# Building the adjacency counts of a graph: how the edge keys are written and loaded, and which engine casts a part of them

## The reference

```python
edge_index = jnp.stack([src, dst])
h = jnp.maximum(_layernorm(x, axis=-1), 0.0)
x = x + _L0_gnn_ref(h, src, dst, ...)          # two degree-normed convolutions
h = jnp.maximum(_layernorm(x, axis=-1), 0.0)
x = x + _L1_gnn_ref(h, src, dst, ...)          # two mean aggregations with weights
h = jnp.maximum(_layernorm(x, axis=-1), 0.0)
x = x + _L2_gnn_ref(h, edge_index, ...)        # two attention layers
h = jnp.maximum(_layernorm(x, axis=-1), 0.0)
x = x + _L3_gnn_ref(h, edge_index, 3125)
```

## Time and profile before

| | |
|---|---|
| median of 3 runs | 802.03 us (800.73 to 803.16) |
| the profiled execution's own time | 800.52 us |
| its span | 798.7 us |
| granted TensorE clock, mean of the span | 0.932 |
| PE busy | 700.2 us, 88% |
| DVE busy | 570.8 us, 71% |
| ACT busy | 409.6 us, 51% |
| POOL busy | 39.2 us, 5% |

### The profile page before, as it was taken

The page is one execution under the profiler, slowest core; times in us unless marked ns, Lnnn a source line. Parts: engine busy times, 40 slices in busy tenths (PEclk is TensorE's granted clock), DMA queues, the critical chain, the costliest instruction groups (busy, mean ns, idle before and its releaser), DMA issues. The chain is left out here.

```text
span 798.7 us, 18765 instructions
## 1 busy us (share of the span) xinstructions
PE 700.2 (88%) x7841; PEld 658.5 (82%) x7841; DVE 570.8 (71%) x1273; ACT 409.6 (51%) x699; POOL 39.2 (5%) x30
## 2 busy tenths in 40 slices
PE   6078888789998999999999759999963999997997
PEld 6066655569997999999999749999953999996997
DVE  6198999995355545533444689999878999996732
ACT  6236666661004123222132778999566899974600
POOL 6001352000000000000000000000000000000000
PEclk8688999989998999999999979999965999999999
DMA  5000000006990000000000412666661099997811
GB/s 138 22 1 20 7 7 6 1 2 219 413 412 9 1 2 2 2 2 2 1 27 14 128 37 73 216 213 200 210 214 35 19 207 217 217 178 206 167 28 35
DMA packets 121203, 78.05 MB, mean 98 GB/s; under 512 B 97793, under 2 KB 115905, under 8 KB 120986
## 3 DMA queue, kind: packets, MB, share of 16 engines
q1 hardware_dynamic: 120446, 75.33, 33.1%
q0 software_dynamic: 384, 0.94, 0.4%
q10 hardware_dynamic: 284, 0.51, 0.2%
HBM read 30.51 MB, written 25.78 MB: 70 GB/s over the span
## 5 line engine op out<-in xcount | busy, mean ns | idle before, releaser
L1998 PE MATMUL banks<-loose,adjacency 128*128 128x194 f16 x1250 | 211.9, 247 | 0.0
L773 PE MATMUL banks<-y_sb,adjacency 128*128 128x192 f16 (+1 forms) x1875 | 166.2, 249 | 0.8 <-DVE h_sb L1020 0.8
L773 PEld LDWEIGHTS banks<-y_sb,adjacency 128*128 128x128 f16 x1875 | 161.7, 99 | 1.5 <-DVE h_sb L1020 1.0
L1997 PE MATMUL banks<-x_sb,gat_masks 128*128 128x194 f16 x820 | 141.0, 248 | 2.3 <-DVE adjacency L1912 2.2
L1968 ACT ACTIVATE gat_masks<-y_sb,node_scalars 128x640 bf16<-128x640 f32 x164 | 121.8, 826 | 4.0 <-PEq L135 4.0
L1998 PEld LDWEIGHTS banks<-loose,adjacency 128*128 128x128 f16 x1250 | 122.4, 98 | 0.3
L714 ACT ACTIVATE adjacency<-counts 128x850 f16<-128x850 f32 x92 | 81.0, 880 | 69.6 <-PE counts L607 67.7
L1997 PEld LDWEIGHTS banks<-x_sb,gat_masks 128*128 128x128 f16 x820 | 80.3, 98 | 3.2 <-DVE y_sb L1908 2.6
L1908 DVE TENSOR_TENSOR gat_masks<-gat_masks,adjacency 128x1920 f16<-128x1920 bf16 (+1 forms) x64 | 64.2, 1006 | 6.6 <-ACT gat_masks L1968 6.4
L1251 ACT ACTIVATE y_sb<-banks 96x256 f32<-96x256 f32 x50 | 19.1, 381 | 93.7 <-PE banks L1283 93.7
L431 DVE TENSOR_TENSOR hot_codes<-codes_iota,unpacked 128x2016 f16<-128x2016 f16 (+5 forms) x76 | 65.3, 909 | 0.2
(11 more groups left out here) (283 smaller groups left out, 1096.8 us busy)
## 6 DMA issues: line engine op xcount, KB each, us to landing
kept_adj<-adjacency SPq DMA_DIRECT2D x5, 4000.0 KB, 31.8
adjacency<-kept_adj SPq DMA_DIRECT2D x25, 800.0 KB, 9.2
y_sb<-a_dst_rows SPq DMA_DIRECT2D x10, 320.0 KB, 3.7
residual<-h_sb SPq DMA_DIRECT2D x5, 240.0 KB, 2.0
kept_x<-x_sb SPq DMA_DIRECT2D x1, 1200.0 KB, 5.1
loose<-residual SPq DMA_DIRECT2D x5, 240.0 KB, 3.6
x_sb<-kept_x SPq DMA_DIRECT2D x5, 240.0 KB, 4.9
x_sb<-in_x SPq DMA_DIRECT2D x4, 240.0 KB
```

The costliest lines, as they stand in the source:

```text
L773: return nc.tensor.matmul(k.ps[:, j % G, 0:cols], k.ADJ[:, i, j * P:(j + 1) * P], y[:, i, 0:cols], start=i == 0, stop=i == NT - 1)
L1997: nc.tensor.matmul(bank[:, 0:2 * BC], over_of(x)[:, q * P:(q + 1) * P], features[0][:, i, :], start=i == 0, stop=False)
L1998: return nc.tensor.matmul(bank[:, 2 * BC:4 * BC], under_of(x)[:, q * P:(q + 1) * P], features[1][:, i, :], start=False, stop=i == NT - 1)
```

## The change

- The write of the keys is cut into three: rows 0 to 47 (`first_keys_out`), 48 to 111 and 112 to 124 (`keys_out`), with each row as one run of 1600 numbers.
- `dst_first` has 112 rows of 250, is loaded first of all, by SyncE's queue, and has a semaphore of its own. DVE does all of the early bases and `early_after` before it turns to `src`; ACT does four of the seven early Sign steps ahead of `dst_scaled`. The early edges come ahead of the main bases.
- The early starts of load 0 and load 1 are summed and released one by one; PE waits for the first before it computes the second.
- DVE's wait for `keys_out` moves from before `unpack(0)` to before `unpack(1)`, after octet 0.
- For loads from the third on, the cast of line 422 goes to ACT, after it has stored the pair that follows the load's turn; DVE waits for it in `unpack`.
- `degree` starts at pair 14, two products after even pairs and one after odd ones, until it has caught up. The main beginnings run over pairs 2 to 9 in quarters of a tile, the shifts over 10 to 13.
- Small: `trouble` is cleared first, its three tests move, `place_of` is waited for.

```diff
-BEGINS_AT, SPLIT_AFTER, SPREAD_AT, STARTS_AFTER, TURN_AT = 4, 3, 8, 4, 17
+BEGINS_AT, BEGINS_IN, SPLIT_AFTER, SPREAD_AT, STARTS_AFTER, TURN_AT = 2, 4, 3, 10, 4, 17
+DEGREES_FROM = 14
-EARLY_EDGES = 224
-FIRST_KEYS = -(-(EP * EARLY_EDGES + P) // EF)
+EARLY_PARTS, EARLY_EDGES = 112, 250
+FIRST_KEYS = 48
+SIGNS_FIRST = 4
...
-    key_writes = 16 * 2
+    key_writes = 16 * 3
...
     def _(sp):
+        sp.dma_start(dst_first, d.dst[0:EARLY_PARTS * EARLY_EDGES].rearrange("(p f) -> p f", p=EARLY_PARTS)).then_inc(first_in, 16)
...
-        for some, done in ((slice(0, FIRST_KEYS), first_keys_out), (slice(FIRST_KEYS, EP), keys_out)):
-            sp.dma_start(d.keys[some.start * EF:some.stop * EF, :].rearrange("(p f) e -> p f e", f=EF),
-                         pairs_f[some, :, :]).then_inc(done, 16)
+        for some, done in ((slice(0, FIRST_KEYS), first_keys_out), (slice(FIRST_KEYS, EVEN), keys_out), (slice(EVEN, EP), keys_out)):
+            sp.dma_start(d.keys[some.start * EF:some.stop * EF, :].rearrange("(p f) e -> p (f e)", f=EF),
+                         pairs_flat[some, :]).then_inc(done, 16)
...
-            pool.wait_ge(starts_ready, 1 if load < EARLY_LOADS else 2)
+            pool.wait_ge(starts_ready, min(load, EARLY_LOADS) + 1)
...
+        def bases(n, parts, first, bias, most):
+
+            chain(dve.tensor_scalar(base_i[0:parts, n:n + 1], first, DIVIDE, None, ALU.mult))
+            chain(dve.tensor_scalar(base_i[0:parts, n:n + 1], base_i[0:parts, n:n + 1], SHIFT, None, ALU.logical_shift_right))
+            chain(dve.tensor_scalar(node_of[0:parts, n:n + 1], base_i[0:parts, n:n + 1], float(W), None, ALU.mult))
+            dve.tensor_scalar(bias[0:parts, :], step_nodes[0:parts, 0:most], node_of[0:parts, n:n + 1], 0.5, ALU.add,
+                              ALU.subtract).then_inc(bias_ready, 1)
+            chain(dve.tensor_scalar(place_of[0:parts, n:n + 1], base_i[0:parts, n:n + 1], float(WT), None, ALU.mult))
...
+        dve.wait_ge(first_in, 16)
+        bases(1, EARLY_PARTS, dst_first[:, 0:1], early_bias, EARLY_STEPS)
+        dve.tensor_scalar(early_after[0:EARLY_PARTS, :], places[0:EARLY_PARTS, 0:LEADING + WT * EARLY_WINDOWS], place_of[0:EARLY_PARTS, 1:2],
+                          None, ALU.is_gt).then_inc(edges_ready, 1)
         dve.wait_ge(src_in, 32)
...
+        dve.wait_ge(signed, EARLY_STEPS)
+        edges_of(EARLY_PARTS, early_signs, early_edges, EARLY_STEPS)
+        dve.wait_ge(dst_in, 32)
+        bases(0, EP, dst[:, 0:1], main_bias, MAIN_STEPS)
...
+        for load in range(EARLY_LOADS):
+            starts_of(slice(load, load + 1), early_starts_ps, load + 1)
...
-            chain.later(dve.tensor_copy(unpacked[:, load % 2, 0, 0:n, :], keys_ps[:, 0:n].unsqueeze(2).to_broadcast([P, n, 2])))
+            if load < EARLY_LOADS:
+                chain.later(dve.tensor_copy(unpacked[:, load % 2, 0, 0:n, :], rows_of(load)))
+            else:
+                dve.wait_ge(rows_cast, load - EARLY_LOADS + 1)
...
-        dve.wait_ge(keys_out, key_writes)
         unpack(0)
...
                 if o == 0:
+                    dve.wait_ge(keys_out, key_writes)
                     unpack(1)
...
         for n in range(EARLY_LOADS):
-            last = start(early_starts_ps[:, 2 * n:2 * n + 2], n, 1, EARLY_WINDOWS)
-        last.then_inc(starts_summed, 1)
+            if n > 0:
+                pe.wait_ge(starts_ready, n)
+            start(early_starts_ps[:, 2 * n:2 * n + 2], n, 1, EARLY_WINDOWS).then_inc(starts_summed, 1)
         keep_busy(BUSY_NEXT)
...
-            if p >= LATER:
-                degree(p - LATER)
-            if BEGINS_AT <= p < BEGINS_AT + 4:
+            if p >= DEGREES_FROM:
+                for _ in range(2 - p % 2):
+                    if degrees_done <= p - LATER:
+                        degree(degrees_done)
+                        degrees_done += 1
+            if BEGINS_AT <= p < BEGINS_AT + 2 * BEGINS_IN:
...
-                if p == (TURN_AT if load == 1 else FIRST[load] // 2 + 1):
+                if p == turned_at(load):
                     turn(load + 1)
...
-        act.dma_start(dst_first, d.dst[0:EP * EARLY_EDGES].rearrange("(p f) -> p f", p=EP)).then_inc(dst_in, 16)
         act.preload_act_table(ACT.Sign)
-        act.wait_ge(dst_in, 48)
...
+        act.wait_ge(bias_ready, 1)
+        signs_from(dst_first, early_bias, early_signs, range(0, SIGNS_FIRST), EF)
+        act.wait_ge(dst_in, 32)
         nc.scalar.activation(dst_scaled, dst, ACT.Copy, scale=HALF * NT).then_inc(scaled_ready, 1)
...
+        signs_from(dst_first, early_bias, early_signs, range(SIGNS_FIRST, EARLY_STEPS), EF)
...
+            for load in range(EARLY_LOADS, len(LOADS)):
+                if p == turned_at(load - 1) + 1:
+                    act.wait_ge(keys_turned, load + 1)
+                    act.wait_ge(rows_hot, FIRST[load - 1] // OCT)
+                    nc.scalar.activation(unpacked[:, load % 2, 0, 0:LOADS[load] * WT, :], rows_of(load), ACT.Copy).then_inc(rows_cast, 1)
```

More of the change, by code:

```diff
@@ L203, in build_adjacency @@
     dst, src, row_i, tile_i = (early(t, I32, EF) for t in range(4))
-    dst_scaled, dst_first = early(4, F32, EF), early(5, I32, EARLY_EDGES)
+    dst_scaled, dst_first = early(4, F32, EF), early(5, I32, EARLY_EDGES)[0:EARLY_PARTS, :]
     pads = k.ADJ[0:1, 7, 0:4 * P].bitcast(F32)
-    pairs_f = k.h_memory[0:EP, 0:2 * EF].rearrange("p (f e) -> p f e", e=2)
+    pairs_flat = k.h_memory[0:EP, 0:2 * EF]
+    pairs_f = pairs_flat.rearrange("p (f e) -> p f e", e=2)
     def kept(t, n):
@@ L221, in build_adjacency @@
     total_ps = keys_ps[0:1, 0:NT + 3]
+    first_in = sem("first_in")
     dst_in, src_in, x_in, keys_out = sem("dst_in"), sem("src_in"), sem("x_in"), sem("keys_out")
@@ L243, in build_adjacency, with turned_at, rows_of @@
     block = c.enter_context(nc.Block())
-    key_writes = 16 * 2
+    def turned_at(load):
+        return TURN_AT if load == 1 else FIRST[load] // 2 + 1
+    def rows_of(load):
+        n = LOADS[load] * WT
+        return keys_ps[:, 0:n].unsqueeze(2).to_broadcast([P, n, 2])
+    key_writes = 16 * 3
     octs = NW // OCT
@@ L342, in _ @@
             chain.later(dve.memset(edges[:, WT + n:], 0.0))
+        chain.later(dve.memset(trouble[:, :], 0.0))
         chain.later(dve.memset(halves[:, :, :, :], 0.0))
@@ L349, in _, with edges_of @@
         chain.all()
[L351 to L357, removed]
+        def bases(n, parts, first, bias, most):
[5 more added lines that the diff above has]
+            chain(dve.tensor_scalar(place_of[0:parts, n:n + 1], base_i[0:parts, n:n + 1], float(WT), None, ALU.mult))
+        def edges_of(parts, signs_of, edges, n):
+            return dve.tensor_tensor(edges[0:parts, WT - 1:WT + n], signs_of[0:parts, 1:n + 2], signs_of[0:parts, 0:n + 1],
+                                     ALU.subtract).then_inc(edges_ready, 1)
+        dve.wait_ge(first_in, 16)
+        bases(1, EARLY_PARTS, dst_first[:, 0:1], early_bias, EARLY_STEPS)
+        dve.tensor_scalar(early_after[0:EARLY_PARTS, :], places[0:EARLY_PARTS, 0:LEADING + WT * EARLY_WINDOWS], place_of[0:EARLY_PARTS, 1:2],
+                          None, ALU.is_gt).then_inc(edges_ready, 1)
         dve.wait_ge(src_in, 32)
@@ L556, in _, with begin @@
         keep_busy(BUSY_FIRST)
-        def begin(out, after, edges, n, tile, windows, some):
+        def begin(out, parts, after, edges, n, tile, windows, some):
             for at in some:
@@ L562, in begin @@
                 first = LEADING + WT * TILE_WINDOWS * tile - lag
-                last = nc.tensor.matmul(out, after[0:EP, first:first + WT * (windows - 1) + 1:WT], edges[0:EP, at:at + WT],
+                last = nc.tensor.matmul(out, after[0:parts, first:first + WT * (windows - 1) + 1:WT], edges[0:parts, at:at + WT],
                                         start=at == 0, stop=at == n + WT - 1, skip_group_check=True)
@@ L652, in stay_busy @@
                 nc.tensor.matmul(counts[:, 0, 0:P], k.ident_h[:, :], k.ident_h[:, :], start=True, stop=True)
-        for p in range(PAIRS - LATER, PAIRS):
+        for p in range(degrees_done, PAIRS):
             last = degree(p)
```

65 lines of the change are left out of this document (25 added, 40 removed).

## The result

The changed kernel takes 779.72 us in the median of four runs (779.62 to 780.21) against 801.38 us before (798.61 to 803.16): a ratio of 0.9734, 95% interval 0.9705 to 0.9763. The forecast was 779.5 in a range of 775.5 to 786. The profiled execution's span fell from 798.7 to 777.9 us.

The account below looks back on a forecast made before the run. VectorE's 16.8 us wait for the keys' write was taken to bound the matrix building. Gains of 17.65 (start), 2.8 (PE waits) and 1.3 (cast) sum to 21.75 us, giving 778.8 to 780.3; forecast 779.5, range 775.5 to 786.

Parts of the forecast that it names:

- What bound the kernel: Building of the matrix: VectorE waits 16.8 us before the first unpacking for the keys' write, 89 rows in one DMA engine.
- The start: Up to VectorE's unpacking of load 0: at 18.9 us instead of 36.55, a gain of 17.65 us.
- The chain: Steps making the first load: bases 4.3, early edges 9.7, first starts 12.25, gather issued 13.4 and landed 17.4 us.
- `keep_busy`, not the transfer, is late next: Before load 0's transposes: the idle PE products end between 17.7 and 18.4 us, later than the gather at 17.4.
- both my ends of 4.7 and 5.41: Durations in us for the 45 idle products: 4.7 at 0.104 each, 5.41 as in the kernel before.
- my bound of 18.4: Before load 0's transposes: the latest end in us forecast for the 45 idle products, the earliest being 17.7.
- The octet after it: After load 0: the moved wait for the keys comes at 25.1 us; keys and main Signs are ready, nothing held up.
- The old waits for PE: In the counting: VectorE's two waits for PE, 2.8 us together, are removed; ends 0.8 and 2.8.
- The cast: In the counting: ACT's casts save VectorE 1.5 us, the third load loses 0.2 net; gain 1.3, ends 0 and 1.8.
- the write was spread: Keys' write: the rival said 64 rows still use one DMA engine, start gain 10 us, 787 us; chance 0.05.
- the late chain: Rival at the start: `dst_first` lands late or the gather is longest, VectorE starts at 22 to 23.7, 782.5 to 784.5; chance 0.14.
- PE at the lower clock: Rival in the counting: PE idles at 1.2 GHz and sets the pace, 25 us lost, about 803; chance 0.03.

Follow-up runs that it names:

- the even pieces alone: The kernel before, with only the writes of the keys cut into 48, 64 and 13 rows: 785.62 us, ratio 0.982.
- the old ones: The changed kernel with the two old writes of the keys, rows 0 to 35 and 36 to 124: 789.5 us, ratio 0.9892.
- 61 rows: The changed kernel with the second write of the keys cut at 61 rows and the third with 16: 786.27 us.
- The first profile: Profile of the changed kernel's first group of runs, against the kernel before; median 779.72 us, ratio 0.9734.
- second group of runs: The changed kernel run again with no edit, against the kernel before on the same chip: 781.28 us, ratio 0.9749.

## Why the prediction was right, and where it was not

- **What bound the kernel** was read rightly: the even pieces alone bring 14.2 us, the old ones cost 8.2 to 10.9 under the new order, and 61 rows behave as 89 did.
- **The start**: forecast 18.9, measured 17.53, 19.0 us of gain instead of 17.65. The chain held to 0.3 us at the bases, the early edges, the first starts and the first gather (4.3 for 4.37, 9.7 for 9.52, 12.25 for 11.99, 13.4 for 13.12). The keys went out at 9.26, 0.4 before the forecast, as VectorE's codes took 1.10 us and not 1.57, and the gather took 3.1 us at most, not 4. The step that was off is "`keep_busy`, not the transfer, is late next": the 45 products took 3.74 us, less than both my ends of 4.7 and 5.41. I had taken the pace of the full clock from the first 60, 0.104 each, but those ran at two paces. In the trace of the kernel before they start 0.153 us apart up to 4.6 us and 0.079 apart behind that, though the view by stretches gives a clock of 1.00 for both parts. Its 45 products, the 5.41 us, were such a mixture too. At 0.079 apart 45 take 3.6 us, at 0.153 they take 6.9, and both my ends lay between. VectorE's own statistics, over at 17.6 for the forecast's 18.1, were last instead. In five other profiles the products did decide, with load 0 at 18.2 to 20.1, and in two of them they ended at 19.7, beyond my bound of 18.4: I had priced no 45 products nearly all at the lower clock (6.53 us). The first profile, with the full clock here, was a lucky one.
- **The octet after it**: right. No wait for the keys or the Signs; load 1 is unpacked at 23.73, for the forecast's 25.1 less the 1.4 of the start.
- **The old waits for PE**: 2.8 us went and 0.42 came before octet 5. The reason given, less work in PE, is not borne out in its part on the degrees: with them in place from pair 2 there was no wait either, though PE then had the full clock. That leaves the later shifts and the smaller beginnings, which no run undid one by one, so the cause is open here.
- **The cast**: forecast 1.3, worth 0.4. The saving was right (0.32 a load, six loads, ACT's own price 0.36 and not 0.48); the term mis-sized is the wait for the third load, 1.24 and not 0.5. The 5.7 us of some executions come mostly from the late gather, for which the prediction had no term. PE was at the lower clock until 48 us, which I had kept for a rival and priced over the whole counting only.
- The two errors, 1.4 too little at the start and 1.2 too much in the counting (4.1 forecast, 2.94 measured), cancel. For the profiled execution the sum gave 778.8, and it took 779.72, as the layers behind were 1.2 us longer. That 779.5 stands so close to 779.72 is luck in part; the same kernel's second group of runs had a median of 781.28.
- **Rivals**: the write was spread; the late chain did not happen; PE at the lower clock did happen for most of the time from 22 to 48 us, and in the first profile cost at most the 0.42 before octet 5 and a part of the 1.24.

## What to carry to other kernels

Look at the DMA share in a stretch where everything waits: 0.06 is one of sixteen engines, and then the number of rows of the transfer is the thing to change, not the wait. A wait that is removed hands the path to the next thing that was hidden. Here that was, in part of the executions, work put in only to occupy an engine, so price such work at both clocks. And when the runs of a kernel scatter, take more than one profile: two of them, laid side by side, named two sources here, the idle products and the third gather.

## What was not expected of the hardware

- GpSimd's indirect gather of 120 rows takes 0.98 to 1.2 us when VectorE is idle or in its one-input statistics. While VectorE runs two-input f16 instructions back to back it took 1.13 to 1.36 us for three gathers of the kernel before, but 2.73, 6.58 and up to 7.93 us for others. In the fourteen profiles all those of 6.57 us and more end 0.85 to 0.95 us behind the moment at which VectorE leaves this work. In this kernel it makes a second time for the same code, 5.7 against 1.2 us of waiting at the third load.
- Taking products out of PE lowered its clock: with the degrees the granted clock was 1.00 from 30 to 48 us, without them 0.63, 0.50 and 0.50 (1.2 GHz for most of it; 0.50 to 0.72 in the second profile of the changed kernel), and 33 idle products just before the stretch changed little after 30 us (0.57, 0.50, 0.51).
- The same 45 products took 3.74, 5.39 and 6.53 us in three executions, with the same order of instructions up to there: they start 0.079 us apart at a granted clock of 1.00 and 0.153 apart at 0.50. The clock was 1.00 throughout in the first, 0.50 until about 16 us in the second and until about 19 us in the third.
